# Expert weights fetched with the token rows, shared-expert outputs added by GpSimd, and two row blocks of the down projection computed side by side

## The reference

```
x = x + tanh(g_xattn[l]) * attention_l(layernorm(x), ctx, ctx)
x = x + tanh(g_ffn[l])   * ffn_l(layernorm(x))

ffn_l(h):                           # h: 2048 tokens x 512
  scores = softmax(h @ w_gate)      # layer 0: 8 experts;  layer 1: sigmoid, 32 experts
  topk_w, topk_i = top_k(scores)    # layer 0: 2,  layer 1: 6;  weights divided by their sum
  routed = sum_k topk_w[k] * down[e_k](silu(h @ gate[e_k]) * (h @ up[e_k]))    # width 256 / 192
  shared = silu(h @ sg) * (h @ su) @ sd                                        # width 1024 / 384
  return routed + shared
```

## Time and profile before

| | |
|---|---|
| median of 3 runs | 2045.34 us (2045.24 to 2046.21) |
| the profiled execution | 2046.07 us, of which 2044.0 us are the profile's span |
| busy in the span | PE 1886.2 us (92%), DVE 1348.0 (66%), ACT 1145.5 (56%), POOL 782.2 (38%) |
| mean granted TensorE clock | 0.969 of full speed |
| FFN 0, shared expert | from 446.6 us to about 728 us |
| FFN 0, routed experts | about 728 to 905 us |
| FFN 1, shared expert | from 1369.9 us to 1535.3 us |
| FFN 1, routed experts | 1535.3 us to the end |

### The profile page before, as it was taken

How to read it: one execution, slowest core, us unless ns; L and a number is a source line. 1 busy time by engine, 2 the same in 40 slices (tenths; PEclk the granted TensorE clock), 3 DMA queues, 4 the chain that set the end, 5 groups by cost and what they waited for, 6 DMA issues and landing times. The chain is left out here.

```text
span 2044.0 us, 40829 instructions
## 1 busy us (share of the span) xinstructions
PE 1886.2 (92%) x10024; PEld 1220.2 (60%) x10025; DVE 1348.0 (66%) x2556; ACT 1145.5 (56%) x1857; POOL 782.2 (38%) x941
## 2 busy tenths in 40 slices
PE   5999999989999999994999999987888999999998
PEld 2333333344888878872433333345667888888886
DVE  6899988841445544436889988859984555555553
ACT  1777777753322335541777777762224566666664
POOL 3222222125201125553222222127644656565555
PEclk9999999999999999995999999988999999999998
DMA  4422222142111458665422222131027888888886
GB/s 141 119 59 64 61 66 64 40 172 97 55 55 56 144 175 196 139 107 138 123 67 59 65 60 67 45 136 39 1 96 180 190 196 203 194 201 201 204 186 107
DMA packets 100082, 233.53 MB, mean 114 GB/s; under 512 B 17410, under 2 KB 20484, under 8 KB 99972
## 3 DMA queue, kind: packets, MB, share of 16 engines
q1 hardware_dynamic: 61572, 137.75, 23.7%
q0 software_dynamic: 33792, 79.71, 20.1%
q10 hardware_dynamic: 4608, 14.68, 2.2%
HBM read 127.23 MB, written 57.67 MB: 90 GB/s over the span
## 5 line engine op out<-in xcount | busy, mean ns | idle before, releaser
L599 DVE TENSOR_REDUCE maxima<-ring_ps 128x1 f32<-128x512 f32 x1024 | 639.8, 681 | 89.2 <-PE ring_ps L386 88.2
L493 ACT ACTIVATE probs<-score_ps 128x1024 f32<-128x1024 f32 x512 | 501.8, 1019 | 91.6 <-PE score_ps L403 89.3
L386 PE MATMUL ring_ps<-k_turned,q_turned 64*128 64x512 f32 x1024 | 414.3, 481 | 39.7 <-DMA q_turned<-q_lo 18.4
L386 PEld LDWEIGHTS ring_ps<-k_turned,q_turned 64*128 64x128 f32 x1024 | 179.0, 193 | 367.1 <-DVE maxima L599 258.0
L1179 PE MATMUL bank_f<-w_gu_parts_f,xg_T_f 128*128 x1800 | 367.1, 352 | 2.1 <-issue 2.1
L1179 PEld LDWEIGHTS bank_f<-w_gu_parts_f,xg_T_f 128*128 128x128 f32 x1800 | 325.8, 190 | 30.4 <-issue 3.0
L403 PE MATMUL score_ps<-q_turned,k_turned 64*128 64x512 f32 x1024 | 336.3, 447 | 1.7 <-ACT probs L493 1.4
L420 PE MATMUL out_ps<-probs,v_ones 128*32 128x512 f32 x2048 | 273.3, 606 | 10.7 <-issue 10.4
L1204 PE MATMUL bank_f<-w_dn_parts_f,hg_T_f 96*128 (+1 forms) x888 | 243.6, 410 | 1.5 <-DVE hg_T_f L1773 1.5
L983 POOL DMA_INDIRECT xg_f<-xh_rows_f,idx_in_f x156 | 159.5, 1022 | 186.1 <-DVE idx_in_f L1663 106.7
L999 POOL DMA_INDIRECT out_x<-y_tok_f,idx_out_f x111 | 177.2, 1596 | 133.0 <-ACT y_tok_f L1407 94.6
(11 more groups left out here) (232 smaller groups left out, 2335.2 us busy)
## 6 DMA issues: line engine op xcount, KB each, us to landing
w_gu_f<-in_L_w_gu SPq DMA_DIRECT2D x64, 384.0 KB
q_turned<-q_hi SPq DMA_DIRECT2D x128, 128.0 KB, 2.6
w_raw_f<-in_L_w_sh_gu ACTq DMA_DIRECT2D x28, 512.0 KB, 3.5
w_dn_f<-in_L_w_dn SPq DMA_DIRECT2D x32, 384.0 KB
k_turned<-k_hi SPq DMA_DIRECT2D x128, 64.0 KB, 2.1
q_turned<-no_max SPq DMA_DIRECT2D x64, 128.0 KB, 2.6
q_turned<-q_lo SPq DMA_DIRECT2D x64, 128.0 KB, 2.7
w_gu_f<-in_L_w_gu SPq DMA_DIRECT2D x16, 512.0 KB
```

What stands on the lines that cost most here:

```text
L386: pe.matmul(ring(k, "max", i), q_turned[rows, slot, h // 2, c * P:(c + 1) * P], k_turned[rows, slot, :], start=True, stop=True).then_inc(m ...
L493: act.activation(probs[:, (TPB * u + c) % PROBS, pair, :, :], score_ps[:, pair, :, :], ACT.Exp, scale=float(D) ** -0.5).then_inc(exped, 1)
L599: dve.tensor_reduce(maxima[:, par, col:col + 1], ring(k, "max", i), AX.X, ALU.max).then_inc(max_taken, 1)
```

## The change

Three things are changed.

1. **The weights leave the table.** Rows of `xh_rows` and of `xg` get E more columns (8 or 32 floats), which hold the token's combine weight for every expert. SP stores them once (`weight_made`, `weight_stored`). The one-hot tile matrix is then 128x128, multiplied by the token number alone, with a `tensor_scalar`; `entry`, `chosen` and `weights_of` go, and `table_sum` has 128 moving columns in place of 384. In the routed stage ScalarE, right after x_hi(i), loads the tile's expert from the schedule and copies that column of `xg` to `table_sb` (`weight_taken`); the gather into that half of `xg` waits for it.
2. **Readers of the shared outputs.** In layer 1 the outputs of groups 1 and 2 are read as those of group 0 are: by ScalarE, behind `shared_x_hi` and `shared_w_hi` of the next group, and added by GpSimd, in its list behind the first 7 slot matrices of the next group. Group 3, and groups 1 to 3 of layer 0, stay with VectorE. VectorE now makes the low parts of the next group ahead of the next tile matrices.
3. **Down projection.** Blocks 0 and 1 are computed side by side, slice by slice, and then blocks 2 and 3 one after the other.

```diff
-        xh_rows = dram("xh_rows", (ROWS, H))
+        xh_rows = dram("xh_rows", (ROWS, H + E))
+    SOFT_GROUPS = 1 if layer == 0 else B - 1
...
+            sp.wait_ge(weight_made, 1)
+            sp.dma_start(xh_rows[0:TOK, H:H + E].rearrange("(n p) e -> p n e", p=P), weight[:]).then_inc(weight_stored, 16)
...
-                sp.wait_ge(y_read, TPB * b + TPB)
+                if b < SOFT_GROUPS:
+                    sp.wait_ge(y0_added, TPB * b + TPB)
+                else:
+                    sp.wait_ge(y_read, TPB * b + TPB)
...
             for n in range(HOTS, PAIRS):
+                for g in range(1, SOFT_GROUPS):
+                    if n == g * GU + HOTS:
+                        for c in range(TPB):
+                            add_y0(TPB * g + c)
                 slot_one_hot(n)
             pool.wait_ge(table_ready, 1)
+            pool.wait_ge(weight_stored, 16)
+            pool.wait_ge(y0_added, TPB * SOFT_GROUPS)
...
                 pool.wait_ge(xg_turned, i + 3)
+                pool.wait_ge(weight_taken, i + 3)
                 gather(i + 4, half)
...
-                mm = pe.matmul(bank[:, TABLE_BANK, 0:3 * P], slot_hot[:, n % HOTS, :],
-                               tile_hot[:, n % HOTS, :, :].rearrange("p c t -> p (c t)"),
+                mm = pe.matmul(bank[:, TABLE_BANK, 0:P], slot_hot[:, n % HOTS, :],
+                               tile_hot[:, n % HOTS, :],
...
-                for c in range(TPB):
-                    if g > 0 or c >= 2:
-                        pe.wait_ge(y_read, TPB * g + (c - 1))
-                    for f in range(FC):
-                        if c == 0:
-                            pe.wait_ge(h_done, g * FC + f + 1)
+                if g > 0:
+                    pe.wait_ge(y_read, TPB * g)
+                for f in range(FC):
+                    pe.wait_ge(h_done, g * FC + f + 1)
+                    for c in range(2):
+                        down_part(c, f)
+                for c in range(2, TPB):
+                    pe.wait_ge(y_read, TPB * g + (c - 1))
                     for f in range(FC):
+                        down_part(c, f)
...
+            def outputs(g):
+                for c in range(TPB):
+                    act.wait_ge(y_done, TPB * g + c + 1)
+                    if g >= 1:
+                        act.wait_ge(y0_added, TPB * g + (c - 3))
+                    act.activation(y0(c), bank[:, 6 + c % 2, :], ACT.Copy, scale=gate[:, 0:1]).then_inc(y_read, 1)
...
                 if f + 1 == FC and g + 1 < B:
                     shared_x_hi(g + 1)
                     shared_w_hi(n + 1)
+                    if g < SOFT_GROUPS:
+                        outputs(g)
...
                 act.activation(xg_T[:, half, 0, :, :].rearrange("p d m -> p (d m)"), bank[:, 6, :], ACT.Copy).then_inc(xg_hi, 1)
+                expert = act.value_load(sched[0:1, bass.ds(i, 1), 0:1].rearrange("a i c -> a (i c)"), min_val=0, max_val=E - 1)
+                act.activation(table_sb[:, bass.ds(i, 1), 1:2].rearrange("p a c -> p (a c)"),
+                               xg[:, half, bass.ds(expert + H, 1)], ACT.Copy).then_inc(weight_taken, 1)
...
-            then(dve.tensor_copy(entry[:, :, :, 0], token_f[:, :, None].to_broadcast([P, TT, K])))
-            def weights_of(first):
...
-                dve.scalar_tensor_tensor(tile_hot[:, n % HOTS, :, :], count_f[:, None, :].to_broadcast([P, 3, P]),
-                                         tile_of[:, i, k:k + 1],
-                                         entry[:, i, k, :, None].bitcast(F32).to_broadcast([P, 3, P]),
-                                         ALU.is_equal, ALU.mult).then_inc(tile_hot_made, 1)
+                dve.tensor_scalar(tile_hot[:, n % HOTS, :], count_f[:], tile_of[:, i, k:k + 1], token_f[:, i:i + 1],
+                                  ALU.is_equal, ALU.mult).then_inc(tile_hot_made, 1)
...
-            weights_of(0)
             shared_x_lo(1)
             shared_w_lo(FC, 0)
             shared_w_lo(FC, 1)
-            for k in range(KS, K, KS):
-                tile_one_hots(HOTS)
-                weights_of(k)
+            tile_one_hots(HOTS)
...
                 if g + 1 < B:
+                    shared_x_lo(g + 1)
+                    for o in range(2):
+                        shared_w_lo(n + 1, o)
                     tile_one_hots(used + HOTS)
-                    shared_x_lo(g + 1)
                 for c in range(TPB):
-                    if g + 1 < B and c < 2:
-                        shared_w_lo(n + 1, c)
-                    dve.wait_ge(y_done, TPB * g + c + 1)
...
+                    if g >= SOFT_GROUPS:
+                        dve.wait_ge(y_done, TPB * g + c + 1)
...
-                    if c + 1 == TPB and g + 1 < B:
-                        tile_one_hots(used + HOTS_AHEAD)
```

65 lines of the change are left out of this document (26 added, 39 removed).

## The result

The changed kernel takes 2034.67 us, median of 4 runs (2031.39 to 2035.9), the kernel before beside it 2045.78 us. The ratio is 0.9943, with a 95% interval of 0.9931 to 0.9956: faster by 11 us, where 26 were forecast. The profiled execution's span is 2032.2 us, against 2044.0.

A forecast was written before the change was run, and what follows sets the result against it. VectorE was taken to hold layer 1's shared expert, TensorE to bound layer 0's shared expert and layer 1's routed stage. Terms -1.8 - 28.4 + 2.5 + 0.5 = -27.2 us gave 2019 us; own range 2014 to 2026, 8 in 10: 2009 to 2035.

The forecast's parts named there:

- What bounds the kernel: Whole kernel: TensorE bounds layer 0's shared expert and layer 1's routed stage; the slack lies in layer 1's shared expert.
- Start and group 1: Layer 1's shared expert: lighter VectorE work lets gate and up of group 1 end at 1435, not 1446; -11.0 us.
- Down projections: Layer 1, behind groups 1 and 2: ScalarE reads block 0 sooner, so they shorten by 7.4 and 6.8 us.
- The additions: GpSimd, layer 1: 1.3 to 2.4 us each, three hidden by the down projection, the fourth covered by 7 stocked matrices.
- The routed stage: Layer 1: ScalarE's load and copy, 0.64 us per step, mostly fit its wait; some gathers come late; +2.5 us.
- gather loop: Rival, routed stage: the loop outgrows two steps, 9.0 to 9.6 us against 8.8; total 2048 us; chance 0.10.
- Layer 0, table matmuls: Shared expert: 32 matmuls with 128 columns in place of 384 take 0.117 us each, not 0.175; -1.9 us.
- Order: Layer 0's shared expert, groups 1 to 3: the new down projection sequence stalls 0.35 us each; +1.05 us.
- Group 0: Layer 0's shared expert: 96 down matmuls go from 22.7 us to a pace of 0.223 each, less a stall; -0.9 us.
- Layer 0's routed stage: ScalarE's load and copy and the gather's wait cost +0.5 us there, since its steps are longer.
- Faster GpSimd: Rival, layer 1's shared expert: slot matrices fall to 0.6 us each, TensorE sets the pace; 2013 us; chance 0.13.
- Only the down projections gain: Rival, layer 1: groups 2 and 3 stay as they are, group 1 gains only 5 us; 2026 to 2033; chance 0.24.

The follow-up runs named there:

- weights_alone: The full change without the new readers of the shared outputs and the new down projection order; 0.9926 of the kernel before, median 2029.56 us.
- downs_alone: The full change with the weights through the table as before (384 columns), new readers and down projection order kept; 1.0018 of the kernel before.
- outputs_back: The full change, VectorE again reading and adding layer 1's outputs of groups 1 and 2, layer 0's table matmul streaming one matrix three times; 0.9967 of before.
- no_additions: The full change without GpSimd's eight additions of groups 1 and 2 in layer 1, those outputs left out; 0.9904 of the kernel before.

## Why the prediction was off, point by point

It said 2019 us and the kernel takes 2034.67: outside its own range of 2014 to 2026, and by 0.3 us inside the range for 8 in 10. That it got so near is in part luck, since 4.0 us of gain at the start of layer 1 that it hadn't counted stand against 16.7 us of misses. Two slips in its sums change nothing: 2018.9 less 0.7 is 2018.2, and 20.2 against 21.0 is -0.8.

- **What bounds the kernel** was read rightly: the gain lies in layer 1's shared expert (-25.4 us of 28.4), VectorE's tile matrices and `weights_of` were what held it, and TensorE's stages of layer 0 and the routed stage could only lose.
- **Start and group 1**: 15.0 us in place of 11.0. Gate and up of group 1 gave 10.5 (36.03 to 25.58), as forecast, and group 0's down projection 4.7 (16.39 to 11.65), which the forecast left at nothing. The last silu came at 1435.6, the forecast's 1435, although the stage began 4.5 us later: two errors that cancel. weights_alone shows that the gain belongs to the weights' part alone (61.0 us, downs_alone 76.1).
- **Down projections**: 9.8 us for the 9.7 of the working, both times. But counted by itself a shorter down projection is no gain: downs_alone and outputs_back show that its time was also the others' time to fill their stocks.
- **The additions**, the step that failed in layer 1: "TensorE has 7 matrices in stock, 4 us of work", and gate and up of group 3 at -0.7 us. The prediction priced them in GpSimd's list alone, and let three of four be hidden. It left out that they stand beside VectorE's low parts and tile matrices, which take twice as long then, so that tile matrices, not slot matrices, run out; group 3 cost 5.3 us more than before. Its bound for uncovered additions (10 us) was close to what no_additions gave back, 9.0 us in the two gate and up stages.
- **The routed stage**, the largest miss: the term of 0.64 us of ScalarE per step that "fits into the 0.96 us for which ScalarE waits" came to 9.0 us in place of 2.5. The fit was judged at one place of the step where nothing is split; at the two places shown above ScalarE's slack was 94 us in 420, about 95 steps, and load and copy took 39 of it. The load was also priced too low, 0.44 against some 0.6 with its address. The risk was named in the wrong form: the rival "gather loop" counted on the gather's wait for the copy, which without a load is worth 0.4 us, nothing that can be read.
- **Layer 0, table matmuls**: the upper bound "if the weight load sets the pace" was the truth, and a little short: 0.19 us against 0.17, which with the slower end of group 3 makes +1.1 in place of -1.9. **Order**: the stall's term was 1.05, measured 1.5. **Group 0**: -0.9 foreseen, -0.1 measured; 96 matmuls take 22.7 and 22.6 us, 0.236 each in both kernels, so what the forecast took for a wait is their pace here. Its 0.223 was an average that takes in the shorter table matmuls; 16 gate and up matmuls take 3.66 us, 0.229 each. **Layer 0's routed stage**: +1.8 against +0.5, but it is 187.5 to 192.2 us over all kernels, with no order by copy or load (191.0 without the copy), so the difference isn't read as an effect.
- **Rivals.** Faster GpSimd: 29 slot matrices took 19.86 us in group 2, 0.685 each, so it didn't come. "Only the down projections gain" gives 2026 to 2033 us, near the measured time, and one of its conditions is what happened in another form: the additions outlasted a stock, that of tile matrices. But its main point is refuted: the shorter down projections alone gain nothing (downs_alone), and group 1 was the part that gained.

## What to carry to other kernels

A phase that one engine spends waiting may be the phase in which the others fill their buffers: before shortening it, add up each engine's work over the whole period, not over the phase. An instruction moved to an idle engine must be priced with what runs beside it, on both sides. And in a ring of steps, price not only an added instruction but the queue's work for it (a loaded number, an address from a register), against the slack of that engine in all steps; an experiment that doubles it shows quickly whether there is any.

## What the hardware showed that was not expected

- A load of a number from the schedule, 282 ns by its own record, cost 7 to 12 us in 111 tiles (0.06 to 0.11 each) the first time and 10 to 14 (0.09 to 0.13) the second; a copy of 194 ns from a fixed column cost nothing that can be read.
- A table matmul of 128 columns took 0.19 us of TensorE's time, one of 384 columns 0.17, and one of 384 columns that reads one matrix three times 0.25.
- A 128x512 subtraction of VectorE took 0.69 us alone and 1.79 beside a 128x512 addition of GpSimd, which went from 1.27 to 1.74. Tile matrices took 0.27 us alone and 1.27 beside group 0's additions, which stayed at 1.26. Beside GpSimd's 128x128 slot matrices both VectorE instructions kept nearly their time (0.69 and 0.30).
